# A two-norm, convolution-gated mixture of experts on one core: GpSimd's waits in the last router round, and the order of the first two rounds

## The reference

```python
x = x + conv_gate(ln_c(x))      # ln_c: mean and variance over the 64 channels
# conv_gate(z) = z * sigmoid(conv3x3([max_c(z), mean_c(z)]) + b)
t = tokens(x)                   # (B, H*W, 64)
t = t + moe(ln_t(t))            # ln_t: again over the 64 channels
# moe(z): p = softmax(z @ router_w + router_b); the two largest, scaled to sum 1
#         sum over both: p_k * (z @ expert_w[k] + expert_b[k]), 8 experts
```

## Time and profile before

| | |
|---|---|
| median of 3 runs | 1438.6 us (1438.05 to 1440.72) |
| the profiled execution | 1439.05 us, span 1437.3 us |
| PE busy | 1348.2 us (94%) |
| DVE busy | 1243.6 us (87%) |
| ACT busy | 1045.9 us (73%) |
| POOL busy | 1067.9 us (74%) |
| mean granted clock of PE | 0.97 |
| chain that ended last | PE 66%, DVE 14%, issue 8%, POOL 2%, ACT 2% |

### The profile page before, as it was taken

The page is one execution under the profiler, slowest core; times in us unless marked ns, Lnnn a source line. Parts: engine busy times, 40 slices in busy tenths (PEclk is TensorE's granted clock), DMA queues, the critical chain, the costliest instruction groups (busy, mean ns, idle before and its releaser), DMA issues.

```text
span 1437.3 us, 33101 instructions
## 1 busy us (share of the span) xinstructions
PE 1348.2 (94%) x11750; PEld 631.9 (44%) x11750; DVE 1243.6 (87%) x1527; ACT 1045.9 (73%) x3949; POOL 1067.9 (74%) x659
## 2 busy tenths in 40 slices
PE   8864999999999999999999999999999988999998
PEld 8853444444444444444444444444444322333332
DVE  6786799978998899988999889988998898987776
ACT  6666888878888788878888888888888333443432
POOL 5334787887788787887787777886878886887765
PEclk9955999999999999999999999999999998999999
DMA  6442466656667666566667666576665555556563
GB/s 222 135 119 65 142 193 206 196 185 208 196 192 217 186 202 209 174 212 193 193 181 213 187 208 198 172 229 190 198 207 155 154 154 144 164 171 189 170 190 116
DMA packets 85877, 259.97 MB, mean 181 GB/s; under 512 B 13776, under 2 KB 13776, under 8 KB 85712
## 3 DMA queue, kind: packets, MB, share of 16 engines
q1 hardware_dynamic: 85712, 257.85, 59.6%
HBM read 206.42 MB, written 51.38 MB: 179 GB/s over the span
## 4 chain that ended last, share of the span: by engine, by line
PE 66%; DVE 14%; issue 8%; POOL 2%; ACT 2%; DVEq 0%; POOLq 0%; ACTq 0%
PE moe L551 38%; PE gb L497 13%; DVE gx L693 10%; PE tm L476 8%; PE tm L490 2%; PE moe L545 2%; PE tm L536 2%; PE tm L575 1%; DVE u L778 1%; DVE oh L728 1%; POOL dl L1215 1%; DVE ot L706 1%; ACT gs L980 1%; ACT sq L942 0%; POOL parts L1171 0%
## 5 line engine op out<-in xcount | busy, mean ns | idle before, releaser
L551 PE MATMUL moe<-gx,wc 128*64 128x448 f32 x3584 | 813.8, 554 | 0.0
L693 DVE TENSOR_TENSOR gx<-gb,xd 128x896 f32<-128x896 f32 x672 | 710.6, 1085 | 101.2 <-PE gb L497 97.2
L1165 POOL TENSOR_TENSOR gx<-gs,xd 128x896 f32<-128x896 f32 x224 | 489.3, 2185 | 269.0 <-ACT gs L980 213.8
L980 ACT ACTIVATE gs<-gb 128x896 f32<-128x896 f32 x224 | 205.4, 917 | 219.7 <-PE gb L497 218.7
L942 ACT ACTIVATE sq<-xct 112x64 f32<-112x64 f32 x1400 | 338.1, 244 | 7.6 <-DVE early_s L680 2.1
L551 PEld LDWEIGHTS moe<-gx,wc 128*64 128x64 f32 x3584 | 218.5, 136 | 233.0 <-issue 200.8
L497 PE MATMUL gb<-s,cg 52*128 52x448 f16 x1792 | 259.4, 357 | 42.1 <-DVE gx L693 34.4
L942 ACT ACTIVATION_READ_ACCUMULATOR sq<-xct 112x1 f32 x1400 | 263.3, 188 | 0.0
L1181 POOL TENSOR_TENSOR tt<-xc,a1s 128x896 f32<-128x896 f32 x112 | 236.2, 2109 | 11.2 <-issue 9.5
L497 PEld LDWEIGHTS gb<-s,cg 52*128 52x128 f16 x1792 | 56.8, 94 | 378.0 <-DVE gx L693 316.8
L476 PEld LDWEIGHTS tm<-rhs,xa 64*112 64x112 f32 x2800 | 170.8, 182 | 32.7 <-issue 19.0
(11 more groups left out here) (94 smaller groups left out, 1094.7 us busy)
## 6 DMA issues: line engine op xcount, KB each, us to landing
xd<-in_x_dram SPq DMA_DIRECT2D x448, 224.0 KB, 4.0
xa<-in_x_dram SPq DMA_DIRECT2D x112, 448.0 KB, 4.5
xc<-in_x_dram SPq DMA_DIRECT2D x112, 448.0 KB, 4.8
out_dram<-ot SPq DMA_DIRECT2D x112, 448.0 KB, 3.6
gx<-in_const_g_dram SPq DMA_DIRECT2D x1, 384.0 KB, 4.8
cf<-in_const_f_dram SPq DMA_DIRECT2D x1, 333.5 KB, 2.8
gx<-in_L_ffn_expert_w_dram SPq DMA_DIRECT2D x1, 128.0 KB, 4.6
cf<-in_L_ffn_expert_b_dram SPq DMA_DIRECT2D x8, 2.0 KB
```

The costliest lines, as they stand in the source:

```text
L551: last = pe.matmul(moe[b * CH:(b + 1) * CH, c, 0:HALF], wc[:, k * CH:(k + 1) * CH], gx[:, u, b, :], start=False, stop=(k == KT - 1), skip_ ...
L693: dve.tensor_tensor(gx[:, i, :, :], gb[:, 2 * slot:2 * slot + 2, 0:HALF], xd[:, v % 2, :, c * HALF:(c + 1) * HALF], ALU.mult).then_inc(sca ...
L980: act.activation(gs[:, j, :, :], gb[:, 2:4, 0:HALF], ACT.Copy).then_inc(gate_out, 1)
L1165: pool.tensor_tensor(gx[:, ND + j, :, :], gs[:, j, :, :], xd[:, v % 2, :, j * HALF:(j + 1) * HALF], ALU.mult).then_inc(scaled_p, 1)
```

## The change

In round 8 a second table, `TAIL_END`, replaces `PLACE_END`: GpSimd waits in all sixteen router places 12 to 27 for the end of DVE's work in that place. In round 0 ACT squares the first half of every step and GpSimd the second half of all 14 steps, and GpSimd's constants are made between those squares. SP issues the first tile of `xa` ahead of `wr`, and four tiles of it ahead of the constants. ACT squares one column of ones at its start. In round 1 ACT's `gate_of_conv` goes from step 2 to step 3 and its `router` behind the second half's read-out. The diff, cut to its core:

```diff
+EARLY_LOADS = 4
 EARLY = 6
 JOIN = 6
-ACT_STEPS = 7
...
         def squared_at(r, step, n):
             if r == 0:
-                return QUADS * min(step, ACT_STEPS) + (n if step < ACT_STEPS else 0)
-            if r >= PAIRS:
-                return QUADS * (ACT_STEPS + (PAIRS - 1) * STEPS)
-            return QUADS * (ACT_STEPS + (r - 1) * STEPS + step) + n
+                return step * QUADS // NGRP + min(n, QUADS // NGRP)
+            steps = min(r, PAIRS) * STEPS + (step if r < PAIRS else 0)
+            return QUADS * steps - STEPS * QUADS // NGRP + (n if r < PAIRS else 0)
...
+        TAIL_END = {1: "t_a1", 2: "y_a1", 3: "r1", 6: "v2", 7: "t_a2", 8: "y_a2", 9: "rho"}
+        HALF_END = ("top", "ge", "key_max", "dl", "d", "ge2", "key_max2", "oh2")
+        for place in range(16):
+            TAIL_END[12 + place] = f"{HALF_END[place % 8]}_{place // 8}"
         def vector_place(eng, r, place):
-            if 1 <= r <= PAIRS and place in PLACE_END:
-                b_done(eng, r, B_DVE, PLACE_END[place])
+            ends = TAIL_END if r == PAIRS else PLACE_END
+            if 1 <= r <= PAIRS and place in ends:
+                b_done(eng, r, B_DVE, ends[place])
...
-            sp.dma_start(cf[:, :], const_f).then_inc(ld_first, 16)
-            sp.dma_start(wr[0:CH, :], router_w).then_inc(ld_first, 16)
-            sp.dma_start(wr[CH:P, :], router_w).then_inc(ld_first, 16)
...
-                        begin = (2 if r == 0 else 0) if step == 0 else step + lead
+                        begin = (EARLY_LOADS if r == 0 else 0) if step == 0 else step + lead
...
+            sp.dma_start(cf[:, :], const_f).then_inc(ld_first, 16)
             load_a(0, 0)
-            load_a(0, 1)
+            sp.dma_start(wr[0:CH, :], router_w).then_inc(ld_first, 16)
+            sp.dma_start(wr[CH:P, :], router_w).then_inc(ld_first, 16)
+            for step in range(1, EARLY_LOADS):
+                load_a(0, step)
...
-            dve.memset(ones[:, :], 1.0)
+            dve.memset(ones[:, :], 1.0).then_inc(setup_ones, 1)
...
             def channel_sum(r, step, g):
-                if r == 0 and step >= ACT_STEPS:
-                    dve.wait_ge(pool_squared, NGRP * (step - ACT_STEPS) + g + 1)
+                if r == 0 and g == 1:
+                    dve.wait_ge(pool_squared, step + 1)
...
+            act.wait_ge(setup_ones, 1)
+            act.activation(sq[:, 0, 0:1], ones[0:W, :], ACT.Square)
             act.wait_ge(setup_dve, 1)
...
-                    if r == 0 and step > ACT_STEPS + 1 or r == 1 and step < 2:
-                        act.wait_ge(pool_squared, NGRP * (r * STEPS + step - 1 - ACT_STEPS))
+                    if r == 0 and step > 1 or r == 1 and step < 2:
+                        act.wait_ge(pool_squared, r * STEPS + step - 1)
...
-            def early_body(r, Bp):
+            def first_body():
+                for step in range(STEPS):
+                    centred_to_sbuf(0, step, 0)
+                    square_group(0, step, 0)
+                    centred_to_sbuf(0, step, 1)
+                    if step == JOIN:
+                        join_early(0)
+
+            def second_body(r):
                 for step in range(STEPS):
                     centred_to_sbuf(r, step, 0)
-                    if Bp or step < ACT_STEPS:
-                        square_group(r, step, 0)
-                    if Bp and step == 2:
+                    if step == 3:
                         gate_of_conv(r)
-                    if Bp:
-                        router(r, step)
+                    square_group(r, step, 0)
                     centred_to_sbuf(r, step, 1)
-                    if Bp and step % 2 == 0 or not Bp and step < ACT_STEPS:
+                    router(r, step)
+                    if step % 2 == 0:
                         square_group(r, step, 1)
-                    elif Bp:
+                    else:
                         square(r, step, 2)
                         square(r, step, 3)
...
+            def square_group(step):
+                pool.wait_ge(centred_out, a_at(0, NGRP, step, 2))
+                if step > 0:
+                    pool.wait_ge(summed, summed_at(0, step - 1, 1))
+                cols = slice(2 * GRP, 4 * GRP)
+                pool.tensor_tensor(sq[:, cols, :], xct[:, step % 2, cols, :], xct[:, step % 2, cols, :], ALU.mult) \
+                    .then_inc(pool_squared, 1)
...
+            pool.wait_ge(ld_first, FIRST_LOADS)
+            for step in range(STEPS):
+                square_group(step)
+                if step == 1:
+                    pool.wait_ge(ld_const, LOADS)
+                    link(pool.tensor_copy(prio[:, :], prio_in))
+                elif 2 <= step < 8:
+                    setup_of_band(step - 2)
+                elif step == 8:
+                    link(pool.tensor_copy(cg[:, :], cg_load))
+                elif step == 9:
+                    pool.wait_ge(ld_bias, BIAS_LOADS)
+                    setup_of_biases()
...
-            for step in range(ACT_STEPS, STEPS):
-                for g in range(NGRP):
-                    square_group(step, g)
```

More of the change, by code:

```diff
@@ L1045, in router @@
                     widen(r, 1, "2")
-            def early_body(r, Bp):
+            def first_body():
[6 more added lines that the diff above has]
+            def second_body(r):
                 for step in range(STEPS):
                     centred_to_sbuf(r, step, 0)
-                    if Bp or step < ACT_STEPS:
-                        square_group(r, step, 0)
-                    if Bp and step == 2:
+                    if step == 3:
                         gate_of_conv(r)
-                    if Bp:
-                        router(r, step)
+                    square_group(r, step, 0)
                     centred_to_sbuf(r, step, 1)
-                    if Bp and step % 2 == 0 or not Bp and step < ACT_STEPS:
+                    router(r, step)
+                    if step % 2 == 0:
                         square_group(r, step, 1)
-                    elif Bp:
+                    else:
                         square(r, step, 2)
                         square(r, step, 3)
-                    if Bp and step == 8:
+                    if step == 8:
                         affine_to_q(r, 0)
@@ L1106, in body @@
                         square(r, step, 2)
-            early_body(0, False)
+            first_body()
             act.wait_ge(setup_pool, POOL_SETUP)
-            early_body(1, True)
+            second_body(1)
             body(2, True, True)
@@ L1132, in _, with setup_of_band @@
             link(pool.memset(powers[:, 2:3], -0.5))
-            pool.wait_ge(ld_first, FIRST_LOADS)
-            pool.wait_ge(ld_const, LOADS)
-            link(pool.tensor_copy(prio[:, :], prio_in))
-            for n in range(6):
+            def square_group(step):
[5 more added lines that the diff above has]
+                    .then_inc(pool_squared, 1)
+            def setup_of_band(n):
                 for kw in range(3):
@@ L1142, in _, with setup_of_biases @@
                         link(pool.tensor_tensor(band[:, n, :], band[:, n, :], band_part, ALU.add))
-            link(pool.tensor_copy(cg[:, :], cg_load))
-            pool.wait_ge(ld_bias, BIAS_LOADS)
-            link(pool.tensor_copy(bh[:, :], bias_base))
-            link(pool.tensor_tensor(bias_base, bias_base, low_row.to_broadcast([SR, P]), ALU.mult))
-            link(pool.tensor_tensor(bh[:, :], bh[:, :], high_sign.to_broadcast([SR, P]), ALU.mult))
-            link(pool.tensor_tensor(bw[:, :], bias_base, bh[:, :], ALU.add))
-            def square_group(step, g):
-                pool.wait_ge(centred_out, a_at(0, NGRP, step, g + 1))
-                pool.wait_ge(summed, summed_at(0, step - 1, g))
-                cols = slice(2 * GRP * g, 2 * GRP * (g + 1))
-                pool.tensor_tensor(sq[:, cols, :], xct[:, step % 2, cols, :], xct[:, step % 2, cols, :], ALU.mult) \
-                    .then_inc(pool_squared, 1)
+            def setup_of_biases():
+                link(pool.tensor_copy(bh[:, :], bias_base))
+                link(pool.tensor_tensor(bias_base, bias_base, low_row.to_broadcast([SR, P]), ALU.mult))
+                link(pool.tensor_tensor(bh[:, :], bh[:, :], high_sign.to_broadcast([SR, P]), ALU.mult))
+                link(pool.tensor_tensor(bw[:, :], bias_base, bh[:, :], ALU.add))
+            pool.wait_ge(ld_first, FIRST_LOADS)
[11 more added lines that the diff above has]
+                    setup_of_biases()
             def scale_unit(r, v, j):
```

1 line of the change is left out of this document (added).

## The result

The changed kernel takes 1429.43 us by the median (1428.77 to 1430.19, 4 runs) against 1439.14 of the kernel before in the same comparison: a ratio of 0.9932, 95% interval 0.9915 to 0.9949. The prediction was 1428.0 us, range 1424.0 to 1433.5. The profiled execution has a span of 1428.4 us and a mean granted clock of 0.975 (before: 1437.3 and 0.970).

What follows compares the result with a forecast made beforehand. Round 8 was taken as bound by GpSimd blocking VectorE and a fallen clock, round 1 by a ScalarE-VectorE loop, round 0 by TensorE. 7.1 + 0 + 3.5 = 10.6 us off 1439.05 gave 1428.4, median 1428.0, range 1424.0 to 1433.5.

Steps and rivals of the forecast that it cites:

- The block at place 13: Round 8: gapless GpSimd operations keep VectorE's `ge` at 7.08 us instead of 1.08; the odd hold cuts that train.
- Places 13 to 16: Round 8: with the holds, place 16 starts at 1196.6 against 1203.74, 7.1 us; faster 16 to 17 makes 8.3 together.
- Cost of the even holds: Round 8: GpSimd starts 0.7 to 1.0 us later at places 18 and 22, costing 0.1 at 19 and 1.0 at 23.
- The terms behind place 6: Round 1: four steps without the read-out 3.0 us, less VectorE idling 2.3, minus 1.5 for `ge` beside GpSimd's product.
- `sig`: Round 1, step 3: sigmoid ends at 69.0 behind a group's read-out and table load; VectorE, there at 68.8, loses 0.3 us.
- The drain behind the table load: Round 1: by the skill page about 1.38 us more, `sig` another 1.4 later, round 1 giving 2.1; left out of the sum.
- B: Rival, chance 0.10: round 1 gives nothing because its loop is VectorE's; 1431.5 us.
- C: Rival, chance 0.10: the clock falls in round 8's held stalls too, 1 to 3 us per stall; 1429.5 to 1432.
- E: Rival, chance 0.05: round 8's holds chain both engines in a loop of up to 12.7 us a step; 1436.4.
- F: Rival, chance 0.04: the long block returns at places 13 or 21 of rounds 2 to 7, 33 us lost; 1461.
- D: Rival, chance 0.07: the even holds cost nothing and the start is quicker; 1423.5 to 1425.5 us.
- G: Rival, chance 0.02: round 8's holds do nothing because the block forms ahead of them (hand-over); 1433 to 1435 us.

Runs made afterwards that it cites:

- The two pauses: Kernel before, GpSimd waiting at place 13 of round 8 for its own last result: ahead of `gx` 1430.24 us, or between `gx` and `tt` 1435.15 us.
- the single hold: Changed kernel with the holds of round 8 kept at router places 13 and 26 only: 1426.33 us, stretch 83.55.
- without the pause: The combination without its one pause of GpSimd at place 13 of round 8: 1435.33 us (12 runs).
- the part alone: Kernel before with only ScalarE's new order in round 1 (`gate_of_conv` in step 3, `router` behind the second read-out): 1433.83 us.
- the combination: Changed kernel without round 8's new holds, GpSimd pausing ahead of `gx` at place 13, round 1's sigmoid ahead of group (3,0)'s read-out: 1425.51 us.

## Why the prediction was right, and where it was not

- **The block at place 13: right, and shown.** The cause named was a train of GpSimd operations without a gap. The two pauses show it without GpSimd waiting for VectorE: `ge` lasts until shortly after the first gap, at either of the two spots. What the prediction did not see is that `ge` could also get in ahead of `lg`, as it did in one profile of fourteen. The reading of the Trainium skill against which this was weighed, "SBUF — State Buffer", section on the two separate sides, as a hand-over at each instruction's end, would have had `ge` end one operation after it asked; by its 7.08, 5.03 and 2.97 us it did not. That whoever starts first has the pair and the other one blocks does agree: `lg` took 2.60 when `ge` was first.
- **Places 13 to 16: 19.2 us predicted, 19.07 measured**, the clock stayed up over idles of 1.18 and 1.56 us, and place 17 followed in 5.09. The 8.3 us of gain was right, by its steps.
- **Cost of the even holds: 1.1 predicted.** At places 22 to 24 1.0 predicted, 0.95 measured (12.68 against 11.73); at 18 to 20 0.1 predicted, 0.25 measured. The hold at 14 stood in the walk from 13 to 16, as an `oh` blocked to 1191.5, but not as a cost of its own; taking it away gave 0.9. That is why the holds cost 2.1 and not 1.1 when they were removed. The sum as written, 8.3 - 1.1, is 7.2 and not 7.1, and free even holds would make 8.3 by it; the bound of 9.3 has 1.0 more, without a term for it, and the single hold then reached it (92.88 - 83.55), which the hold at 14 accounts for.
- **Round 8, 7.1 predicted, 7.15 in the profile, 5.9 by the medians of the holds alone.** Here the profile before was taken for the kernel before. Where the long block stands, the stretch is not one number: 92.88 in it, 90.72 with the new loads, 89.67 with the new round 1, 93.65 without the pause, by where the clock falls and whether a second block follows at place 15. Where it does not stand, the five profiles with all the holds agree within 0.2 (85.57 to 85.75). The gain was taken from a costly execution, the time after it was stable. That 7.1 met 7.15 so closely is in part luck: both were read against that same execution.
- **Round 1: 3.5 predicted, 2.39 in the profile after, 3.85 in the profile of that part alone, and 3.6 at the start of round 2's convolution when fast is set against fast and slow against slow.** The terms behind place 6 were predicted at 3.0 + 2.3 - 1.5 = 3.8 and came out at 4.3 (64.68 us from place 6 to round 2 before, 60.39 after, 60.41 in the part alone). **The step that was mis-sized is `sig`: 0.3 late was predicted, 1.90 was measured.** From the start of the convolution to place 6 it was 7.81 us before, 8.34 in the part alone and 9.69 after: 0.5 is the new order, with the group and the load ahead of `sig`; the other 1.35 goes with the convolution and the group behind it, at slow matmuls (4.79 and 1.45 us where they took 4.15 and 1.01). The old order pays for slow matmuls as well: 8.74, 9.08 and 9.04 us in the three profiles in which it met them. So of the 1.6 that the prediction missed, 0.2 belong to the change and the rest to the moment at which the matmuls turned fast in each profile. A further 0.46 was lost at the start of round 2 in the profile after (17.70 us to the convolution against 17.24), where matmuls were slow for longer; the part alone has 17.26.
- **The drain behind the table load**, which by the Trainium skill, "ScalarE: Activation LUTs", What ACT_TABLE_LOAD costs, would have come on top, is not there: the load begins at 68.91, takes 1.28, and `sig` starts at 70.21.
- **Round 0 and the first loads: 0 predicted, 0 measured.** The first centring matmul came at 6.74 instead of 6.45, within the stated -0.7 to +0.6, and the first matmuls of round 1 stand at 50.12 us in both profiles. GpSimd did fall behind: its squares of steps 2 to 8 come at 16.89 to 36.90 us, 3.34 a step against 2.985, so 2.1 us in six steps where up to 2.9 was allowed. VectorE waited 0.66 and 0.87 us for it, TensorE not at all. Putting the old loads back changed nothing beyond a run's spread (1429.96, one run).
- **The rivals.** B and C did not happen (round 1 gave, and the clock stayed up over idles of up to 1.57 us). E's step of 12.7 us did come twice (12.66 and 12.67 from `tt` to `tt`, at places 14 to 16 and 22 to 24), which is the cost of those even holds; the other five steps took 10.25 to 11.18, so it was no loop, and the seven took 79.6 us instead of 88.9. F did not happen: the lead of 1.93 us at the convolution of round 2 is 1.71 at place 12 of round 8. D's premise that the even holds cost nothing is wrong by 2.1 us. Nor did G: at the odd places it is VectorE that releases `gx`, and `ge` is short.

The sum of 10.6 came out at 8.86 between the two profiled executions (1439.05 and 1430.19): 7.15 in round 8 and 1.71 ahead of it. The missing 1.8 are the sigmoid's 1.6, the 0.5 that came back behind it, 0.46 at the start of round 2, and 0.2 on the way to round 8. The median of the changed kernel lies 0.76 below its profiled execution, where 0.45 was allowed, so the forecast missed it by 1.4 only; that last 0.3 is luck.

## What to carry to other kernels

When a VectorE operation with two SBUF operands takes several times its own length, look at whether GpSimd runs operation after operation without a gap across it; a wait of GpSimd for its own last result (a gap of 0.08 us here) lets VectorE in. GpSimd then stands only for the rest of VectorE's operation (0.7 us here). Put a wait only where the trace shows the train: fourteen further holds, which wait for VectorE's results, cost 2.2 us here; further pauses were not tried. And a stall that drags the clock down is priced as a range, not as the one execution shows it: the stretch with the stall varied by 4 us over four profiles of different kernels, the one with all holds by 0.2 over five. Before two profiles are subtracted, look whether both met the slow or the fast matmuls at the same place: here that hid 1.7 of 3.6 us.

## What the runs showed of the hardware that was not expected

- **Who wins the pair is a matter of hundredths of a microsecond.** Timelines of both engines at place 13: in the kernel with round 1 alone `ge` is shown from 1173.46 and `lg` from 1173.68, and `ge` took 7.03; in the combination they are shown from 1173.46 and 1173.67, and `ge` took 1.20. The GpSimd operation ahead of both ended at 1173.74 in the first and at 1173.71 in the second. The order of the starts doesn't tell the winner; the durations do. `ge` lost to `lg` in thirteen of the fourteen profiles, the seven with a hold at place 13 among them, since the hold stands behind `lg`.
- **Matmuls can be slow where the records show the full clock.** In the convolution of round 1 the column of the granted clock says 1.00 while eight of the matmuls take 3.00 us; in round 2 all twelve take 2.52. Whether that is a clock that the records don't show, or something else, no run here tells. Busy time by stretch, profile after:

```profile
61.00:64.00 3.00, 2.99 (x8) 2.54 (x9) 0.50 (x1) 0.00 (x0) 0.00 (x0) 1.00 0.00 0
67.00:68.00 1.00, 1.00 (x20) 1.00 (x18) 0.00 (x0) 0.00 (x0) 0.00 (x0) 1.00 0.00 0
```
